# Edge coefficients made beside the propagation instead of beside the counting, in a two-layer graph network on one core

## The chip, the core and the metric

The kernel runs on one core of one Trainium2 chip. TensorE (PE) multiplies; VectorE (DVE), ScalarE (ACT) and GpSimd (POOL) work element by element; SyncE (SP) and POOL issue the transfers. Each engine takes its instructions in program order, and engines wait for one another through semaphores. The metric is the time of one execution in microseconds, the median of the runs.

## The reference

The input is a graph of 3125 nodes with 128 features and 50,000 edges sorted by `dst`. Two graph layers follow one another, each on the normalized features and added to them.

```python
h = relu(layernorm(x)) @ W_in + b_in
deg = segment_sum(ones, row);  w = deg^-1/2[row] * deg^-1/2[col]      # row = src, col = dst
cur = acc = h
for _ in range(3):                                                    # propagation
    cur = segment_sum(cur[col] * w, row);  acc = acc + cur
x = x + (acc / 4) @ W_out + b_out

W_rel = einsum('rb,bio->rio', w_comp, weight)                         # 64 edge types from 16 bases
msg = (relu(layernorm(x)) @ W_rel[etype])[src] * norm
x = x + relu(segment_sum(msg, dst) + h_bias + relu(layernorm(x)) @ loop_weight)
```

For the second layer an edge needs 16 coefficients: the row of `w_comp` for its type, times its `norm`. These are the edge coefficients of the title.

## The kernel before, in words

**Set-up (to 54 us).** Edges lie in 391 tiles of 128, and nodes in 200 windows of 16. A pair is one tile in one window; there are 590 pairs, taken ten at a time in 59 turns. Small tables, made from `dst`, tell each engine what belongs to a turn: `tab_count` holds four words a turn for PE (which PSUM bank each pair adds into, and how many banks must have come free), `tab_end` the pair with which a window ends, in 16 bits.

**Counting (54 to 316 us)** builds the 3200 x 3200 matrix of edge counts, `CT`. For each half turn (five pairs) DVE writes one-hot rows of the edges into one of three half buffers (`onehots`, L757 for five pairs at once and L762 for each). PE multiplies them, pair by pair, into a ring of six PSUM banks, one for each open window (`count_pairs`, L1000). Before it starts a group of pairs (3, 2, 3 and 2 of a turn) it waits for the one-hots and for banks. ACT copies two finished windows at a time to `stage` (L1235) and clears the banks (L1237, `copy_windows`); SP sends them to `CT`. In the last ten turns PE also adds up degrees from finished parts of `CT` (`add_degrees`).

The first 49 turns each also make the coefficients of eight tiles: POOL loads their types, spread over the partitions, into one of three buffers `cbuf` (L520); DVE turns them into one-hots of the type (`type_rows`, L727); PE multiplies with `wc_parts`, `w_comp` in three bf16 parts (L1008); DVE sums the three parts (`sum_parts`, L733) and multiplies by `norm` (`finish_coefs`, L741); POOL stores the result to DRAM (L531). These steps stand between the pairs of the turn on DVE and PE.

**Propagation (321 to 486 us)** has three layers of 25 groups of nodes, a group being 25 products of 128 x 128 with 128 x 192 (L1079). Groups are taken in six blocks of 5, 5, 5, 4, 4 and 2. PE works ahead: it may start a block when DVE has read the block before last out of PSUM (`prop_read`). DVE's chain for a block (L845 to L853, then `thirds`, L808 to L811) reads the sums, scales them and writes the operands of the next layer. In layer 3 the products with `W_out` and the second normalization follow (`between_blocks`).

**Second layer (498 to 985 us)**: POOL gathers a tile of rows at a time (L565), DVE makes operands (L881, L884) from coefficients and rows, PE adds up pairs (L1155, `sum_pairs`) and closes groups (L1135). **End**: PE turns the results back, DVE adds `x2` in seven parts (`add_x2`, L899), SP stores.

The order on every engine is written out by hand; there is no scheduler.

Of the kernel before, what the change touches and what calls it, by code (L numbers as in the profile page):

```python
# [41 lines left out]
P = 128  # L42
# [30 lines left out]
GROUPS = ((0, 3), (3, 5), (5, 8), (8, 10))  # L73
FREE_SHIFT, FREE_MASK = 9, 0xFF
# [3 lines left out]
COEF_MM = 6  # L78
COEF_TYPES, COEF_SUM, COEF_OUT = 4, 7, 9
# [13 lines left out]
CT_TURNS = -(-NT // CCH)  # L93
H_TURNS = -(-NG // 4)
# [63 lines left out]
def build(nc, x, src, dst, etype, norm, W_in, b_in, W_out, b_out, weight, w_comp, h_bias, loop_w, out):  # L158
    assert TURNS * U == S
    ctx = ExitStack()  # L160
    with ctx:
# [19 lines left out]
        tab_count = sb("tab_count", [1, TURNS, len(GROUPS)], I32)  # L181
# [13 lines left out]
        coef_sum = sb("coef_sum", [P, CCH * BASES], F32)  # L195
        coef_out = sb("coef_out", [P, HALVES, CCH * BASES], F32)
# [7 lines left out]
        tab_end = sb("tab_end", [1, NW // 2], U16)  # L204
# [13 lines left out]
        cbuf = rings[:, half:half + HALVES * CHALF].rearrange("p (b e) -> p b e", b=HALVES)  # L218
# [18 lines left out]
        mv2 = carve_keys(NG * 2).rearrange("p (g k) -> p g k", g=NG)  # L237

# [29 lines left out]
        words = carve(TURNS * len(GROUPS))  # L268
# [79 lines left out]
        coef_st = [sem(f"coef_st{b}") for b in range(HALVES)]  # L348
# [48 lines left out]
        def _(sp):  # L397
# [53 lines left out]
            for b in range(NB):  # L451
                if b == NB - 2:
# [4 lines left out]
                    for b3 in range(HALVES):  # L457
                        sp.wait_ge(coef_st[b3], 16 * ((CT_TURNS + 2 - b3) // HALVES))
# [39 lines left out]
        def _(pool):  # L498
# [14 lines left out]
            for u in range(U):  # L513
                pool.memset(weights[:, 0, u:u + 1], float(1 << BANK_BITS * (u % HU % 3))).then_inc(pool_c, 1)
                pool.memset(weights[:, 1, u:u + 1], float(1 << BASE + u - 1) if u else 0.0).then_inc(pool_c, 1)

            def load_types(c, b):
                lo = c * (CCH * P)
                span = slice(lo, lo + CCH * P) if isinstance(c, int) else ds(lo, CCH * P)
                pool.dma_start(cbuf[:, b, :], types_dram[span].rearrange("(h e) -> h e", h=2).unsqueeze(0)  # L520
                               .broadcast_to([TYPES, 2, CHALF])).then_inc(et_in[b], 16)

            def reload_types(c, b):
                pool.wait_ge(coef_mm, c - (HALVES - 1))
                load_types(c, b)

            def store_coefs(c, b):
                pool.wait_ge(coef_cp, c + 1)
                at = c * (CCH * BASES)
                span = slice(at, at + CCH * BASES) if isinstance(c, int) else ds(at, CCH * BASES)  # L530
                pool.dma_start(coef_dram[:, span], coef_out[:, b]).then_inc(coef_st[b], 16)  # L531

            pool.wait_ge(types_st, 16)
            for c in range(HALVES):
                load_types(c, c)
            reload_types(HALVES, 0)
            assert (CT_TURNS - 1 - HALVES) % HALVES == 0
            pool.addr_align(BLOCK, offset=0, max_nops=0)
            with pool.Fori(0, (CT_TURNS - 1 - HALVES) // HALVES) as q:
                for j in range(HALVES):  # L540
                    reload_types(q * HALVES + (j + 1 + HALVES), (j + 1) % HALVES)
                    store_coefs(q * HALVES + j, j)
            for c in range(CT_TURNS - HALVES, CT_TURNS + 1):
                store_coefs(c - 1, (c - 1) % HALVES)


            pool.wait_ge(prop_done, 1)
            pool.memset(wout2[:], 0.0).then_inc(out_zero, 1)
# [33 lines left out]
        def _(dve):  # L582
# [97 lines left out]
            word_of = lambda i: words[0:1, :].rearrange("p (n i) -> p n i", i=2)[:, :, i]  # L680
            for i, (lo, hi) in enumerate(GROUPS[0:2]):
                step(dve.tensor_reduce(word_of(i), halves_of(moved[:, 0])[:, :, lo:hi], AX.X, ALU.add), i == 1)
            for i, (lo, hi) in enumerate(GROUPS[0:2]):
                step(dve.scalar_tensor_tensor(word_of(i), halves_of(ws_s)[:, :, hi - 1], float(1 << FREE_SHIFT), word_of(i),
                                              ALU.mult, ALU.add), i == 1)
            step(dve.tensor_single_scalar(tab_count[:].rearrange("p c i -> p (c i)"), words[0:1, :],
# [38 lines left out]
            def type_rows(c, b, loaded):  # L725
                dve.wait_ge(et_in[b], loaded)
                dve.tensor_scalar(cbuf[:, b, :], cbuf[:, b, :], typ[:, 0:1], None, ALU.is_equal).then_inc(typed, 1)  # L727

            def sum_parts(c):
                dve.wait_ge(coef_mm, c + 1)  # L730
                if not (isinstance(c, int) and c == 0):
                    dve.wait_ge(coef_cp, c)
                dve.tensor_reduce(coef_sum[:], ps[:, COEF_BANK, 0:CCH * BASES * PARTS].rearrange("p (n k) -> p n k", k=PARTS),  # L733
                                  AX.X, ALU.add).then_inc(coef_read, 1)

            def finish_coefs(c, b, stored):
                dve.wait_ge(coef_read, c + 1)
                if stored is not None:
                    dve.wait_ge(coef_st[b], stored)
# [6 lines left out]
            def onehots(c, phase, loaded=None, stored=None, coefs=True):  # L746


                for u in range(U):
# [15 lines left out]
                    if u == COEF_SUM and coefs:  # L765
                        sum_parts(c - 1)
# [586 lines left out]
```

## Time and profile before

| | us |
|---|---|
| median of 3 runs | 1008.39 (1006.3 to 1008.63) |
| the profiled execution | 1009.44 |
| its span, first to last instruction | 1007.9 |
| busy in the span: PE / DVE / POOL / ACT | 810.3 / 738.4 / 446.9 / 356.8 |
| mean granted TensorE clock | 0.93 of full |

The rows further down are from the one profiled execution. In a timeline a row is a run of like instructions: start, time covered, engine, line, operation, output and input, count, and in brackets the idle time before it with what ended it. A row of the table by stretches gives the stretch, for each engine its busy time and, in brackets, the number of instructions, then the granted clock of TensorE as a share of full, the share of the DMA engines and GB/s.

### The profile page before, as it was taken

The page shows a single profiled execution, that of the slowest core. Times are in us where ns is not written, and L with a number is a line of the kernel's source. Part 1 is how long each engine was busy: PE and PEld are TensorE (multiplying, and loading weights), DVE is VectorE, ACT ScalarE, POOL GpSimd, SP SyncE. Part 2 cuts the span into 40 slices and gives each one's busy share as a digit, 9 for nine tenths or more (in the row PEclk, how much of TensorE's full clock was granted, in tenths as well). Part 3 has the DMA queues.
Part 4 walks back from the last instruction along what each step waited for, and adds up shares of the span by engine and source line. Part 5 has one row for each costly group of instructions (what it writes and reads, how often), then busy time and mean ns, then how long its engine had stood idle before and what let it go on. Part 6 is the DMA issues. An engine that isn't in the chain of part 4 may idle for free.

```text
span 1007.9 us, 27188 instructions
## 1 busy us (share of the span) xinstructions
PE 810.3 (80%) x5578; PEld 586.0 (58%) x5583; DVE 738.4 (73%) x2438; ACT 356.8 (35%) x708; POOL 446.9 (44%) x532
## 2 busy tenths in 40 slices
PE   4776777667898999999349889988888888888876
PEld 2622232222455999999237667666666666555544
DVE  7879999999764463534437777777677877887884
ACT  0503457788883000002224454444343332222100
POOL 2013322223100000011277777777777777777771
PEclk8689989999876999999659999999999999999999
DMA  4013345566431000012771111111111111111112
GB/s 120 1 39 82 106 113 132 140 151 154 118 104 51 2 2 1 5 35 85 237 209 52 52 52 54 52 53 52 52 52 52 52 53 54 52 52 52 52 53 77
DMA packets 64848, 73.26 MB, mean 73 GB/s; under 512 B 12803, under 2 KB 53178, under 8 KB 64666
## 3 DMA queue, kind: packets, MB, share of 16 engines
q1 hardware_dynamic: 48362, 37.30, 13.6%
q0 software_dynamic: 16432, 35.29, 12.5%
q8 instruction: 27, 0.44, 0.2%
q14 instruction: 27, 0.22, 0.1%
HBM read 43.85 MB, written 8.22 MB: 52 GB/s over the span
## 4 chain that ended last, share of the span: by engine, by line
PE 36%; DVE 23%; issue 15%; DVEq 9%; POOL 8%; DMA 7%; ACT 2%; SPq 1%; ACTq 0%; POOLq 0%
PE ps L1079 15%; PE ps L1155 10%; POOL CT L565 8%; DMA CT<-h_dram,src_col 5%; PE ps L1000 5%; DVE ohbuf L762 5%; DVE CT L881 5%; DVE CT L884 3%; DVEq L884 3%; DVE u L762 2%; DVEq L124 2%; PE ps L1135 2%; DVE coef_sum L733 2%; DVEq L881 2%; DVE ohbuf L757 1%
## 5 line engine op out<-in xcount | busy, mean ns | idle before, releaser
L565 POOL DMA_INDIRECT CT<-h_dram,src_col x391 | 370.1, 947 | 125.0 <-issue 97.2
L1155 PE MATMUL ps<-CT 128*128 128x256 f32 x1180 | 305.9, 409 | 64.9 <-DVE CT L884 31.7
L1155 PEld LDWEIGHTS ps<-CT 128*128 128x128 f32 x1180 | 206.5, 194 | 158.8 <-issue 140.3
L884 DVE SCALAR_TENSOR_TENSOR CT<-ps,dlP,CT 128x256 f32<-128x256 f32 x580 | 279.9, 483 | 4.3
L881 DVE COPY CT<-CT 128x128 f32 x590 | 148.4, 252 | 124.8 <-PE ps L1155 55.4
L1296 ACT COPY CT<-ps 128x256 f32<-128x256 f32 x200 | 77.7, 388 | 311.2 <-PE ps L1155 297.6
L1000 PE MATMUL ps<-ohbuf 128*128 128x400 bf16 x395 | 118.5, 381 | 37.0 <-DVE ohbuf L762 14.2
L1235 ACT CAST stage<-ps 128x800 bf16<-128x800 f32 x100 | 82.3, 823 | 93.7 <-PE ps L1000 93.3
L520 POOL DMA_DIRECT2D u<-types_dram x49 | 32.5, 668 | 179.3 <-PE ps L1008 166.2
L1079 PE MATMUL ps<-u,CT 128*128 128x192 bf16 x1250 | 105.3, 247 | 0.9 <-DVEq L848 0.9
L1079 PEld LDWEIGHTS ps<-u,CT 128*128 128x128 bf16 x1250 | 103.5, 98 | 2.2 <-DVEq L848 1.1
L762 DVE TENSOR_SCALAR ohbuf<-iota,keys 128x400 bf16<-128x400 int16 x395 | 102.3, 322 | 0.0
L1135 PE MATMUL ps<-CT 128*128 x800 | 95.8, 277 | 6.8 <-ACT CT L1296 4.6
L1135 PEld LDWEIGHTS ps<-CT 128*128 128x128 f32 x800 | 91.2, 192 | 16.7 <-issue 16.7
L1000 PEld LDWEIGHTS ps<-ohbuf 128*128 128x128 bf16 x395 | 39.1, 99 | 105.5 <-issue 82.7
L1237 ACT COPY ps<-zeros 128x800 f32<-128x800 f32 x100 | 83.0, 830 | 8.7
L1000 PE MATMUL ps<-u 128*128 128x400 bf16 x195 | 57.1, 362 | 28.8 <-DVE ohbuf L762 17.2
L1299 ACT COPY ps<-zeros 128x256 f32<-128x256 f32 x200 | 75.2, 376 | 6.4
L553 POOL TENSOR_TENSOR ohbuf<-ohbuf,keys 128x640 f32<-128x640 f32 (+2 forms) x6 | 7.8, 1312 | 143.3 <-DMA ohbuf<-x 143.3
L1256 ACT ACTIVATE keys<-ps 128x256 f32<-128x256 f32 (+1 forms) x6 | 2.2, 365 | 158.2 <-PE ps L1053 158.2
L1000 PEld LDWEIGHTS ps<-u 128*128 128x128 bf16 x195 | 18.8, 96 | 60.8 <-issue 50.8
L845 DVE COPY stage<-ps 128x320 f32<-128x320 f32 (+2 forms) x18 | 7.8, 436 | 63.0 <-PE ps L1079 62.4
(175 smaller groups left out, 671.9 us busy)
## 6 DMA issues: line engine op xcount, KB each, us to landing
CT<-stage SPq DMA_DIRECT2D x200, 100.0 KB, 3.2
u<-types_dram POOLq DMA_DIRECT2D x49, 128.0 KB, 3.4
CT<-h_dram,src_col POOLq DMA_INDIRECT x391, 2.5
coef_dram<-coef_out POOLq DMA_DIRECT2D x49, 64.0 KB, 3.6
CT<-coef_dram SPq DMA_DIRECT2D x1, 3048.0 KB, 12.2
out<-CT SPq DMA_DIRECT2D x4, 256.0 KB
ohbuf<-x SPq DMA_DIRECT2D x3, 320.0 KB, 4.5
x_dram<-ohbuf SPq DMA_DIRECT2D x3, 320.0 KB, 2.3
```

Of the source, the lines that this page charges most:

```text
L565: pool.indirect_dma_start(out=gring[:, (j + 1) % GRING, :], out_offset=None, in_=h2_dram, in_offset=bass.IndirectOffsetOnAxis(ap=src_col[: ...
L762: dve.tensor_scalar(ohB[h][:, u % HU, :], iota16[:], loP[:, col], None, ALU.is_equal).then_inc(oh_ready, 1)
L881: dve.tensor_copy(gpair[:, u:u + 1, :], gring[:, ds(pairs.place(total, GRING), 1), :]).then_inc(pair_in, 1)
L884: dve.scalar_tensor_tensor(kpair[:, u, :, :], nodes.unsqueeze(1).broadcast_to([P, BASES, WIN]), dl, coef_flat[:, ds(tiles * -BASES + NT * ...
L1000: pe.matmul(bank_of(count_words[at], u - lo), ohA[h][:, u % HU, :], ohB[h][:, u % HU, :], start=False, stop=True, skip_group_check=True).t ...
L1079: ins = pe.matmul(psf[:, at:at + PART], CT[:, k, m * P:(m + 1) * P], u[:, k, :], start=(k == 0 and not onto_zeros), stop=(k == NG - 1), sk ...
L1135: pe.matmul(bank, wrel[:, b, :], rows, start=(b == 0), stop=False)
L1155: pe.matmul(ps[:, ds(summed.place(counts[u][0], RING), 1), 0:WIN * BASES], gpair[:, u, :], kpair[:, u, :, :].rearrange("p b d -> p (b d)") ...
L1235: act.copy(stage[:, 2 * i:2 * i + 2, :], ps[:, bank:bank + 2, 0:LO]).then_inc(staged, 1)
L1237: act.copy(ps[:, bank:bank + 2, 0:LO], zeros[:].unsqueeze(1).broadcast_to([P, 2, LO])).then_inc(slots_free, 2)
L1296: act.copy(zsb[:, half, :, j * WIN:(j + 1) * WIN], ps[:, bank, 0:WIN * BASES].rearrange("p (b d) -> p b d", b=BASES)).then_inc(zcopied, 1)
L1299: act.copy(ps[:, bank, 0:WIN * BASES], zeros[:, 0:WIN * BASES]).then_inc(slots2, 1)
```

## The change

1. The coefficient steps leave the counting turns. They now stand in the propagation: POOL waits for the first scaled rows (`u_ready`) and loads three buffers; `COEF_PLAN` says how many of the 49 coefficient turns stand beside which block of which layer. PE puts up to two coefficient products behind each of a block's last groups (`coefs_after`). DVE cuts types (`type_rows`) and sums parts (`sum_parts`) behind the chain of the block before (`coefs_beside`). The product with `norm` moves from DVE to POOL, where it stands ahead of the load for the third turn after it and of its own store. The buffers move into the free part of `stage`, and there are two PSUM banks for the products instead of one.
2. PE's words for a turn: two (for five pairs each) instead of four. PE waits once for each half turn.
3. `tab_end` is 32 bits wide, and ACT masks each value in a register.
4. Of the last `x2` additions and transposes, five are dealt out between the pairs of the last turn instead of ahead of it.

```diff
-GROUPS = ((0, 3), (3, 5), (5, 8), (8, 10))
+COEF_PLAN = {(0, 2): 3, (0, 3): 4, (0, 4): 4, (0, 5): 2, (1, 0): 6, (1, 1): 6, (1, 2): 6, (1, 3): 4, (1, 4): 4, (1, 5): 2,
+             (2, 0): 6, (2, 1): 2}
...
             pool.wait_ge(types_st, 16)
-            for c in range(HALVES):
-                load_types(c, c)
...
-                    reload_types(q * HALVES + (j + 1 + HALVES), (j + 1) % HALVES)
-                    store_coefs(q * HALVES + j, j)
...
+            pool.wait_ge(u_ready, 1)
+            for t in range(HALVES):
+                load_types(t)
             pool.memset(wout2[:], 0.0).then_inc(out_zero, 1)
+            for t in range(CT_TURNS):
+                b = t % 2
+                pool.wait_ge(coef_read, t + 1)
+                if t >= 2:
+                    pool.wait_ge(coef_st[b], 16 * (t // 2))
+                pool.tensor_tensor(coef_out[:, b].rearrange("p (h i b) -> p i h b", h=2, b=BASES),
...
+                                   .broadcast_to([P, CCH // 2, 2, BASES]), ALU.mult).then_inc(coef_cp, 1)
+                if t + HALVES < CT_TURNS:
+                    pool.wait_ge(coef_mm, t + 1)
+                    load_types(t + HALVES)
+                pool.wait_ge(coef_cp, t + 1)
+                pool.dma_start(coef_dram[:, t * CCH * BASES:(t + 1) * CCH * BASES], coef_out[:, b]).then_inc(coef_st[b], 16)
...
-                    if u == COEF_TYPES and loaded is not None:
-                        type_rows(c, phase, loaded)
-                    if u == COEF_SUM and coefs:
-                        sum_parts(c - 1)
-                    if u == COEF_OUT and coefs:
-                        finish_coefs(c - 1, (phase - 1) % HALVES, stored)
...
+            def types_upto(t):
+                while coef_made[0] < min(t, CT_TURNS):
+                    type_rows(coef_made[0])
+                    coef_made[0] += 1
+
+            def coefs_beside(layer, b):
+                for _ in range(COEF_PLAN.get((layer, b), 0)):
+                    types_upto(coef_made[1] + 2)
+                    sum_parts(coef_made[1])
+                    coef_made[1] += 1
+
             for layer in range(LAYERS):
+                coefs_beside(layer, 0)
                 for b in range(NB):
                     got = layer * NB + b
+                    if (layer, b + 1) in COEF_PLAN:
+                        types_upto(coef_made[1] + 2)
                     dve.wait_ge(prop_done, layer * NG + STARTS[b + 1])
...
+                    coefs_beside(layer, b + 1)
...
-            for i in range(len(OUT_PARTS) - 1):
+            operands(TURNS - 1, nodes=iota16[:, 0:WIN], between=add_x2)
+            for i in range(HU, len(OUT_PARTS)):
                 add_x2(i)
-            operands(TURNS - 1, nodes=iota16[:, 0:WIN])
-            add_x2(len(OUT_PARTS) - 1)
...
+            def coef_products(t):
+                if t >= 2:
+                    pe.wait_ge(coef_read, t - 1)
+                pe.wait_ge(typed, t + 1)
+                for i in range(CCH // 2):
+                    n = 2 * BASES * PARTS
+                    last = pe.matmul(ps[:, 6 + t % 2, i * n:(i + 1) * n], cbuf[:, t % HALVES, i * P:(i + 1) * P],
+                                     wc_parts[:].rearrange("p h b k -> p (h b k)"), start=True, stop=True)
+                last.then_inc(coef_mm, 1)
...
+            def coefs_after(layer, b, done):
+                n = COEF_PLAN.get((layer, b), 0)
+                first = 0 if (layer, b) == (LAYERS - 1, 1) else SIZES[b] - (n + 1) // 2
+                for _ in range(max(0, min(2, n - 2 * (done - first))) if done >= first else 0):
+                    coef_products(next(coef_turn))
```

On PE, the second block of layer 2 stood before as 125 products in one piece:

```order
L1079 MATMUL ps<-ohbuf,CT 128x192 [waits prop_read]
L1079 MATMUL ps<-ohbuf,CT 128x192 x124
```

Now the same block reads as follows (L1075 is a group's products, L997 a coefficient product; `typed` comes from DVE's cutting of types, `coef_read` from its sums).

```order
L1075 MATMUL ps<-ohbuf,CT 128x192 [waits prop_read]
L1075 MATMUL ps<-ohbuf,CT 128x192 x74
L997 MATMUL ps<-wc_parts,stage 128x96 [waits typed,coef_read]
L997 MATMUL ps<-wc_parts,stage 128x96 x3
...
L1075 MATMUL ps<-ohbuf,CT 128x192 x25
```

Six waits for DVE now stand in the block, two behind the third group, two behind the fourth and two behind the fifth; the groups behind them are queued.

On DVE, in the same place, coefficient turns stand between the chain of one block and the chain of the next. L728 sums parts of a turn, L721 cuts the types of the turn two further on, and L829 begins the next chain. `et_in0` to `et_in2` are the loads of the three type buffers.

```order
L728 TENSOR_REDUCE keys<-ps 128x128 [waits dve_c,coef_cp,coef_mm]
L721 TENSOR_SCALAR stage<-stage,typ 128x512 [waits et_in0]
L728 TENSOR_REDUCE stage<-ps 128x128 [waits coef_cp,coef_mm]
L721 TENSOR_SCALAR stage<-stage,typ 128x512 [waits et_in1]
L728 TENSOR_REDUCE keys<-ps 128x128 [waits coef_cp,coef_mm]
L721 TENSOR_SCALAR stage<-stage,typ 128x512 [waits et_in2]
...
L829 COPY stage<-ps 128x320 [waits prop_done]
```

Before, nothing stood between one chain and the next here. Now six sums and six cuts do.

On POOL a coefficient turn is three steps in a row (L535 multiplies by `norm`, L521 loads types, L543 stores).

```order
L535 TENSOR_TENSOR coef_out<-stage,norm_col 128x4x2x16 [waits coef_st0,coef_read]
L521 DMA stage<-types_dram 128x1x512 [waits coef_mm]
L543 DMA coef_dram<-coef_out 128x128 [waits coef_cp]
L535 TENSOR_TENSOR coef_out<-keys,norm_col 128x4x2x16 [waits coef_st1,coef_read]
```

The load of a turn's types, which before waited for PE's product alone, now stands behind the multiplication of the turn three before it, and that one waits for DVE's sum.

## Rows read from the trace of the kernel before

**Rows 1.** Busy time by stretch of counting: PE, PEld, DVE, ACT, POOL, clock, DMA, GB/s.

```profile
58.00:150.00 92.00, 65.67 (x308) 27.10 (x308) 88.99 (x326) 34.75 (x42) 29.23 (x43) 0.93 0.34 91
150.00:200.00 50.00, 34.96 (x168) 14.54 (x168) 49.94 (x183) 35.62 (x44) 13.96 (x24) 0.94 0.54 135
200.00:250.00 50.00, 34.94 (x169) 14.31 (x167) 49.50 (x181) 41.32 (x52) 15.63 (x25) 0.95 0.66 153
250.00:307.00 57.00, 48.81 (x580) 25.88 (x581) 38.69 (x141) 47.30 (x59) 3.59 (x3) 0.80 0.42 110
```

**Rows 2.** Timeline of DVE in counting, a turn with coefficients: its first one-hots, the next turn's.

```profile
77.46 0.49 DVE L757 TENSOR_TENSOR ohbuf<-iota,keys 128x640 bf16<-128x640 int16 x1
...
81.52 0.49 DVE L757 TENSOR_TENSOR u<-iota,keys 128x640 bf16<-128x640 int16 x1
```

**Rows 3.** The same of a turn without coefficients.

```profile
259.49 0.49 DVE L757 TENSOR_TENSOR ohbuf<-iota,keys 128x640 bf16<-128x640 int16 x1 [0.23 <-issue]
...
262.63 0.49 DVE L757 TENSOR_TENSOR ohbuf<-iota,keys 128x640 bf16<-128x640 int16 x1
```

**Rows 4.** Timeline of PE in counting: three turns begin with x3.

```profile
79.18 0.77 PE L1000 MATMUL ps<-ohbuf 128*128 128x400 bf16 x3 [0.69 <-DVE ohbuf L762]
80.15 0.56 PE L1000 MATMUL ps<-ohbuf 128*128 128x400 bf16 x2 [0.20 <-DVE ohbuf L762]
80.90 0.56 PE L1000 MATMUL ps<-ohbuf 128*128 128x400 bf16 x2 [0.20 <-issue]
...
83.67 0.77 PE L1000 MATMUL ps<-u 128*128 128x400 bf16 x3 [1.11 <-DVE u L762]
...
87.70 0.77 PE L1000 MATMUL ps<-ohbuf 128*128 128x400 bf16 x3 [0.70 <-ACT ps L1237]
```

**Rows 5.** Groups by line and form: busy us, mean ns of one, idle before.

```profile
L733 DVE TENSOR_REDUCE coef_sum<-ps 128x128 f32<-128x384 f32 x49 | 27.2, 555 | 0.1
L1008 PE MATMUL ps<-wc_parts,u 128*128 128x96 bf16 x196 | 17.7, 217 | 0.0
L727 DVE TENSOR_SCALAR u<-u,typ 128x512 bf16<-128x512 bf16 x49 | 17.2, 350 | 0.0
L553 POOL TENSOR_TENSOR ohbuf<-ohbuf,keys 128x640 f32<-128x640 f32 x3 | 4.6, 1536 | 117.7 <-DMA ohbuf<-x 117.7
L553 POOL TENSOR_TENSOR ohbuf<-ohbuf,keys 128x256 f32<-128x256 f32 x1 | 0.7, 722 | 6.9 <-DMA ohbuf<-x 6.9
```

**Rows 6.** Type loads: all 49 of L520, then the four between 54 and 70 us.

```profile
DMA to landing us min/median/max: 2.7/3.4/4.1
...
u<-types_dram POOLq DMA_DIRECT2D x4, 128.0 KB, 3.1
```

**Rows 7.** Coefficient stores, all 49 of L531.

```profile
DMA to landing us min/median/max: 2.1/3.6/4.7
```

**Rows 8.** Timeline of DVE in layer 2: first and last of a chain, next chain.

```profile
384.22 0.49 DVE L845 COPY stage<-ps 128x320 f32<-128x320 f32 x1 [6.93 <-PE ps L1079]
...
388.93 0.49 DVE L811 TENSOR_TENSOR u<-stage,u 128x320 bf16<-128x320 f32 x1
394.53 0.49 DVE L845 COPY stage<-ps 128x320 f32<-128x320 f32 x1 [5.11 <-PE ps L1079]
...
413.09 0.42 DVE L845 COPY stage<-ps 128x256 f32<-128x256 f32 x1 [3.05 <-PE ps L1079]
...
416.95 0.43 DVE L811 TENSOR_TENSOR u<-stage,u 128x256 bf16<-128x256 f32 x1
421.34 0.42 DVE L845 COPY stage<-ps 128x256 f32<-128x256 f32 x1 [3.97 <-PE ps L1079]
```

**Rows 9.** Timeline of PE behind the propagation: three products after a wait.

```profile
494.04 1.49 PE L1116 MATMUL ps<-zeros 128*128 128x512 bf16 x3 [4.20 <-DVEq L832]
```

**Rows 10.** Timeline of DVE at the end: first additions, first operands of the last turn.

```profile
986.13 1.29 DVE L899 TENSOR_TENSOR CT<-CT,ps 128x512 f32<-128x512 f32 x2 [2.06 <-PE ps L1178]
...
990.73 0.23 DVE L881 COPY CT<-CT 128x128 f32 x1 [0.58 <-issue]
```

More of the change, by code:

```diff
@@ L267, in build @@
         sixth_i = carve(S).bitcast(I32)
-        words = carve(TURNS * len(GROUPS))
+        words = carve(TURNS * 2)
         tidx_i = carve(TC).bitcast(I32)
@@ L347, in build @@
         coef_cp = sem("coef_cp")
-        coef_st = [sem(f"coef_st{b}") for b in range(HALVES)]
+        coef_st = [sem(f"coef_st{b}") for b in range(2)]
         passed = sem("passed")
@@ L456, in _ @@
                     sp.dma_start(hb[:], h_bias.unsqueeze(1)).then_inc(ld_two, 16)
-                    for b3 in range(HALVES):
-                        sp.wait_ge(coef_st[b3], 16 * ((CT_TURNS + 2 - b3) // HALVES))
+                    for half in range(2):
+                        sp.wait_ge(coef_st[half], 16 * ((CT_TURNS + 1 - half) // 2))
                     sp.dma_start(coef[:, NT - U:NT, :].rearrange("p t b -> p (t b)"),
@@ L865, in _, with operands @@
             pairs = Turn(dve, "pair", NT)
-            def operands(c, first=False, nodes=ps[:, IOTA_BANK, 0:WIN]):
+            def operands(c, first=False, nodes=ps[:, IOTA_BANK, 0:WIN], between=None):
                 row = slice(TURNS - 1 - c, TURNS - c) if isinstance(c, int) else ds(c * -1 + (TURNS - 1), 1)
@@ L887, in operands @@
                                              ALU.is_equal, ALU.mult).then_inc(pair_in, 1)
+                    if between is not None and u % 2 == 1:
+                        between(u // 2)
             operands(0, first=True)
@@ L1157, in sum_pairs @@
                               skip_group_check=True).then_inc(pairs2, 1)
+                    if between is not None and u % 2 == 1:
+                        between(u // 2)
             def complete_groups():
@@ L1187, in _ @@
             assert OUT_PARTS[-2][0] * WPG >= U
-            for i in range(len(OUT_PARTS) - 1):
-                turn_back(i)
-            sum_pairs(TURNS - 1)
+            turn_back(0)
+            turn_back(1)
+            assert len(OUT_PARTS) == HU + 2
+            sum_pairs(TURNS - 1, between=lambda pair: turn_back(pair + 1) if pair else None)
             pe.reg_alu(done_reg, groups_reg, 31, ALU.bitwise_and)
```

153 lines of the change are left out of this document (59 added, 94 removed).

## The prediction

> **What bounds the kernel now.** I read the table by stretches first, then the timelines of DVE and PE in a stretch where nobody rests, then the groups by line, and last the transfers.
>
> In counting, DVE is busy 89.0 of 92, 49.9 of 50 and 49.5 of 50 us up to 250 us, ACT only 34.8, 35.6 and 41.3 [rows 1]. So DVE sets the pace there. From 250 to 307 us it is busy 38.7 of 57, while ACT has 47.3 and PE 48.8; there the ring of banks, ACT's copies and the degree sums hold the turn. A turn with coefficients takes DVE 81.52 - 77.46 = 4.06 us [rows 2], one without 262.63 - 259.49 = 3.14 [rows 3]. In propagation PE is the bound: the reader is to see that DVE waits 6.93, 5.11, 3.05 and 3.97 us ahead of its chains [rows 8], and that five groups take 394.53 - 384.22 = 10.31 us, so 2.06 a group, and a block of four 421.34 - 413.09 = 8.25. DVE's chain for a block of five lasts from 384.22 to 389.42, 5.2 us, for one of four 4.3 [rows 8]. The change thus takes work from a stage where DVE is full and puts it where DVE rests about half the time. The question is whether it can be done there as a side job.
>
> **Counting: -34 us.** DVE sheds 4.06 - 3.14 = 0.92 us in each of 49 turns, 45 us in all; that is the most that can be won. What is late next is PE. Its turns begin at 79.18, 83.67 and 87.70 [rows 4]: 4.49 and 4.03 us. Inside a turn, two pairs and the gap to the next piece take 80.90 - 80.15 = 0.75; a piece of three covers 0.77 and one of two 0.56, so a pair costs 0.21, and the gap between pieces adds 0.75 - 2 x 0.21 = 0.33. Two of the three inner gaps go with the two words, 0.66, and the coefficient products, about 0.2. That leaves 3.63 and 3.17; a loop of three turns has one of the longer kind, so 3.3 on the mean, a little above DVE's 3.14. By stretches [rows 1]:
> - 58 to 150: 92 x (1 - 3.3/4.06) = -17.
> - 150 to 200: 50 x 0.187 = -9, to 41; ACT's 35.6 still fit.
> - 200 to 250: PE would come to 41 too, but ACT has 41.3 of its own and must be handed finished windows; I take 44.5, -5.5.
> - 250 to 307: ACT's 47.3 leave little; -2.5.
>
> Sum -34. Bounds: -45 (all that DVE sheds), and -17 if the long turn starts of PE stay (3.63 us for every turn up to 200 us, 142 x 0.106 = 15, and little after). The wait for five pairs at once lets PE start a half turn only when banks for all its windows are free; this takes from the late stretches and is in the 44.5. The mask on ACT is a register step; two of them, with the waits, fit into PE's gap of 0.33, so at most some 0.15 x 100, hidden while ACT waits; I count nothing. The set-up's few steps fewer I count at nothing too.
>
> **Propagation: +64 us.** The 196 products cost PE little: 17.7 us busy at the most [rows 5], at 0.25 a turn 12. What costs is the ring of dependent steps behind three type buffers. DVE's order is sum t, cut t+2, sum t+1, cut t+3, sum t+2. Cut t+3 needs a load that POOL issues only behind its multiplication of turn t, and that needs sum t. So two turns can't be shorter than this ring:
> - sum 0.56 and cut 0.35 on DVE [rows 5];
> - POOL's multiplication of 128 elements: no row has one so small. 640 take 1.54 us and 256 take 0.72 [rows 5], which is 0.0021 us an element and 0.18 fixed: 0.45. Bounds: 0.31 (a fifth of the row of 640) and 0.72;
> - the load, issue to landing: 3.1 in the quiet stretch from 54 to 70 us, 2.7 to 4.1 over all [rows 6]. Propagation is quiet too, so 3.1;
> - four handoffs, some 0.25.
>
> Together 4.7 us for two turns. The chain of a block comes on top, since DVE does nothing for coefficients during it, and the last cut ahead of it (t+7 behind six turns) waits for its own load. A block of five with six turns takes 3 x 4.7 + 5.2 = 19.3 us instead of 10.3; one of four with four turns 2 x 4.7 + 4.3 = 13.7 instead of 8.25. PE can't run ahead of this: its next groups are queued behind products that wait for `typed`, and DVE gives that only behind the chain. The stalls of PE should be 2 to 4 us each, two or three a block.
> - four blocks with six turns: 4 x 9.0 = 36
> - four with four: 4 x 5.45 = 22
> - the two blocks of two groups, two turns each, at the same 1.4 us a turn: 5.5
> - the three turns of the first block lie where DVE rests and with buffers already full, and this also spares most of the next block's excess, about -5; the last two turns and the delayed rest of the ring at the end give about as much back. Zero.
>
> Sum 64. With loads of 2.7 us it is 24.5 x 0.4 = 10 less, with 4.1 us 24 more; with 2.1, the fastest coefficient store [rows 7] as the nearest row below, 24 less. POOL's bounds give -3 and +7. So 37 to 95. The coefficient stores (two buffers) come due two turns later, 4.7 us or more; the slowest landed in 4.7 [rows 7], so they hold nothing.
>
> One rule speaks against the 3.1. The Trainium skill ("DMA: Bandwidth & Descriptors", section on the anatomy of a DMA from GpSimd) gives about 2.0 us fixed plus bytes by 436 GB/s; for 128 KB my estimate from that page is 2.3 us, and the sum would be 24.5 x 0.8 = 20 smaller, +44. The row has no load that fast, so the row decides.
>
> **End: -2.5 us.** DVE now waits 2.06 us for the first transposes [rows 10] and makes the last turn's operands from 990.73 on. After, operands begin where the wait was and five of seven additions go between them; what the wait held, and an addition behind the last pairs, come off. Bounds 0 and -4.
>
> **Sum.** The profiled execution, 1009.44 us: -34 + 64 - 2.5 gives 1037. The median of before lies 1.05 lower, so 1036 by median; I say 1036.
>
> **The rivals.**
> - *The side job keeps up (faster).* The loads run far enough ahead that PE waits for nothing and only its 12 us remain: 1009.4 - 34 + 12 - 2.5 = 985. For it: DVE rests 3 to 7 us a block [rows 8]. Against it: six turns a block need 1.7 us a turn with DVE's chain in the way, and the ring gives 2.35 without the chain. It decides in favour of faster from an excess below 36 us, which by 24.5 x (3.1 - load) needs loads under 2.0 us; none was seen. 9 in 100.
> - *Quicker loads, the ring still rules.* With loads of 2.3 us, between the fastest store's 2.1 [rows 7] and the fastest load's 2.7 [rows 6], 64 - 24.5 x 0.8 = 44, so 1016. For it: with so little other traffic loads may land sooner than at 54 to 70 us. Against: all 49 took 2.7 or more. 15 in 100. The Trainium skill's figure above would give the same.
> - *PE loses its clock.* Stalls of several us, then products at the lower level of 1.2 GHz. For it: after a wait of 4.20 us three products of 512 columns took 1.49 us [rows 9], which is that level. Against: the stalls here are shorter and come between whole groups, and 25 products of 192 columns in 2.06 us are the full level of 2.4 GHz. A group would take 4.1; a block with six turns 5 x 4.1 + 3 = 23.5 instead of 19.3, one with four 18.4 instead of 13.7; if it holds half of the time, (4 x 4.2 + 4 x 4.7) / 2 = 18: 1054. The Trainium skill ("TensorE: Matmul & The Clock Gate", section on oscillation) describes this for products that wait for transfers every few us; no row of propagation shows it yet. 14 in 100.
> - *Counting gives half.* PE's turn starts stay long: -17, 1053. 8 in 100.
>
> **How the numbers follow.** The forecast has 54 in 100, with 1022 to 1050 as its own range. The range for 8 in 10 goes from 1007, which leaves out the side job that keeps up and the fastest loads, to 1064, which takes in clock or counting but not both with slow loads. About 0.3%, 3 us, is what a measurement of this kernel tells from no change. Slower by more: forecast, clock, counting, and most of the quicker loads, 0.85. Faster: 0.11, the rest 0.04.
>
> **What would show it.** In the profile after: counting ends near 282 us instead of 316; DVE's one-hot turns come every 3.2 to 3.4 us; DVE's cuts (L721) wait 2 to 3 us each for loads; PE's L997 waits for DVE 40 to 50 us in all; the stretch of propagation is some 229 us instead of 165; the load of types lands 3 us after its issue. Wrong would be: loads that land in 2 us, cuts that wait for nothing, or a counting stage that hardly shrinks.

## The result, and the profile after

The changed kernel takes 1038.37 us (median of 4 runs, 1036.69 to 1039.11), the kernel before on the same chip 1007.99 (4 runs): ratio 1.0302, 95% interval 1.0282 to 1.0321, slower by 30 us. The profiled execution took 1037.64 us, its span 1035.8.

The sum of the stages in the two profiled spans is made from four moments: PE's first group of the propagation, DVE's cast of `iota` into `ps` behind it (the end of the propagation), the last operands of turn 58 (the last but one), and the end of the span.

| stage | before, us | after, us | difference | predicted |
|---|---|---|---|---|
| up to the first group | 320.76 | 298.39 | -22.4 | -34 |
| propagation | 173.60 | 228.96 | +55.4 | +64 |
| gather to turn 58 | 489.23 | 487.96 | -1.3 | 0 |
| end | 24.31 | 20.49 | -3.8 | -2.5 |
| span | 1007.9 | 1035.8 | +27.9 | +27.5 |

The windows of the changed kernel over counting, with the columns of [rows 1]:

```profile
58.00:150.00 92.00, 61.81 (x259) 24.86 (x259) 82.51 (x308) 44.25 (x54) 0.00 (x0) 0.98 0.22 58
150.00:200.00 50.00, 31.77 (x137) 12.92 (x136) 44.80 (x168) 43.85 (x55) 0.00 (x0) 1.00 0.42 111
200.00:250.00 50.00, 35.19 (x273) 16.66 (x272) 39.09 (x144) 44.01 (x55) 0.00 (x0) 0.90 0.44 115
250.00:307.00 57.00, 46.40 (x655) 31.70 (x656) 30.01 (x95) 30.38 (x39) 2.39 (x4) 0.67 0.29 77
```

DVE is full no longer: 82.5 of 92 us where it had 89.0. ACT has 44 of 50 us from 150 to 250 us, which is nearly as much as it can: its cast and its clearing copy come round every 1.67 to 1.70 us for most of it, and it waits for PE only 6.8 of the 100 us. The timelines of PE and of DVE in one stretch (answering [rows 2 to 4]) show who has taken DVE's place earlier:

```profile
97.21 1.19 PE L988 MATMUL ps<-ohbuf 128*128 128x400 bf16 x5 [0.91 <-DVE u L743]
98.56 1.16 PE L988 MATMUL ps<-ohbuf 128*128 128x400 bf16 x5 [0.17 <-DVE u L748]
100.99 1.20 PE L988 MATMUL ps<-u 128*128 128x400 bf16 x5 [1.26 <-DVE ohbuf L748]
102.35 1.19 PE L988 MATMUL ps<-ohbuf 128*128 128x400 bf16 x5 [0.16 <-issue]
```

```profile
96.71 0.48 DVE L743 TENSOR_TENSOR u<-iota,keys 128x640 bf16<-128x640 int16 x1
97.11 1.25 DVE L748 TENSOR_SCALAR u<-iota,keys 128x400 bf16<-128x400 int16 x5
98.56 0.49 DVE L743 TENSOR_TENSOR ohbuf<-iota,keys 128x640 bf16<-128x640 int16 x1 [0.21 <-PE ps L988]
```

The half in `u` is ready at 98.36 and PE takes it at 100.99; DVE waits at 98.56 for a buffer that PE has just left. So PE is late, and not for one-hots, although the row names DVE as the last releaser. Between 95 and 106 us PE's turns last 3.4 to 3.8 us, 3.55 on the mean, where the prediction had 3.3.

In the propagation, DVE's waits between 298 and 528 us (us in all, times, longest):

```profile
DVE stage L721 <- DMA stage<-types_dram: 53.7, 34, 2.7
DVE stage L829 <- PE ps L1075: 19.8, 5, 10.0
DVE keys L728 <- PE ps L997: 2.5, 5, 0.8
```

The cuts wait for types 34 times in 49, and the chain (L829) waits for PE five times only, ahead of the first coefficients and behind the last. For the coefficient products the sums (L728) wait 2.5 us in all. DVE, which rested ahead of its chains before [rows 8], now holds PE. The timeline of DVE over one block of five with six turns, from one chain's start to the next:

```profile
385.01 0.48 DVE L829 COPY stage<-ps 128x320 f32<-128x320 f32 x1
...
390.43 0.56 DVE L728 TENSOR_REDUCE keys<-ps 128x128 f32<-128x384 f32 x1 [0.22 <-DVE u L779]
390.90 0.34 DVE L721 TENSOR_SCALAR stage<-stage,typ 128x512 bf16<-128x512 bf16 x1
391.16 0.55 DVE L728 TENSOR_REDUCE stage<-ps 128x128 f32<-128x384 f32 x1
394.37 0.35 DVE L721 TENSOR_SCALAR stage<-stage,typ 128x512 bf16<-128x512 bf16 x1 [2.66 <-DMA stage<-types_dram]
394.64 0.55 DVE L728 TENSOR_REDUCE keys<-ps 128x128 f32<-128x384 f32 x1
...
398.48 0.35 DVE L721 TENSOR_SCALAR stage<-stage,typ 128x512 bf16<-128x512 bf16 x1 [1.70 <-DMA stage<-types_dram]
398.79 0.56 DVE L728 TENSOR_REDUCE keys<-ps 128x128 f32<-128x384 f32 x1
...
402.91 0.48 DVE L829 COPY stage<-ps 128x320 f32<-128x320 f32 x1
```

From chain to chain 17.9 us, where it had been 10.3 [rows 8] and was forecast as 19.3. POOL in the same block:

```profile
395.27 0.41 POOL L535 TENSOR_TENSOR coef_out<-keys,norm_col 128x128 f32<-128x128 f32 x1 [1.12 <-DVE keys L728]
395.63 0.58 POOL L521 DMA_DIRECT2D stage<-types_dram  x1
```

The ring can be read off the two fences: sum at 394.64, multiplication 395.27, load issued 395.63, cut 398.48, next sum of its kind 398.79. That is 4.15 us for two turns. PE in the same block waits for the cut, and then runs slowly for a while (in the window below the granted clock is 0.91):

```profile
387.51 2.23 PE L1075 MATMUL ps<-ohbuf,CT 128*128 128x192 bf16 x25
...
394.87 0.48 PE L997 MATMUL ps<-wc_parts,stage 128*128 128x96 bf16 x4 [3.15 <-DVE stage L721]
395.15 3.44 PE L1075 MATMUL ps<-ohbuf,CT 128*128 128x192 bf16 x25
398.42 0.34 PE L997 MATMUL ps<-wc_parts,stage 128*128 128x96 bf16 x4
```

```profile
321.00:398.00 77.00, 60.72 (x705) 58.90 (x703) 46.72 (x113) 0.00 (x0) 34.84 (x69) 0.91 0.18 58
```

The end, on DVE (answering [rows 10]): the operands of the last turn begin without waiting for a transpose, and the first addition follows behind two pairs.

```profile
1016.34 0.30 DVE L866 COPY CT<-CT 128x128 f32 x1 [0.55 <-PE ps L1155]
...
1017.78 0.69 DVE L886 TENSOR_TENSOR CT<-CT,ps 128x512 f32<-128x512 f32 x1 [0.23 <-PE ps L1180]
```

### The profile page after: what moved, and what is told of

Its sections match the earlier page's. It is cut to its first block, busy times and chain, and to the rows that moved or that the text cites. A ratio compares the mean times of both kernels' runs of the same rounds, so it can differ in the third digit from the quotient of the medians.

```text
span 1035.8 us, 26594 instructions
## 1 busy us (share of the span) xinstructions
PE 798.4 (77%) x5582; PEld 587.0 (57%) x5583; DVE 733.2 (71%) x2387; ACT 355.6 (34%) x708; POOL 457.4 (44%) x581
## 4 chain that ended last, share of the span: by engine, by line
PE 34%; DVE 22%; issue 15%; DMA 10%; DVEq 9%; POOL 7%; ACT 2%; SPq 1%; POOLq 0%; ACTq 0%
PE ps L1155 12%; PE ps L1075 8%; PE ps L988 7%; POOL CT L562 6%; DMA stage<-types_dram 5%; DVE CT L866 5%; DMA CT<-h_dram,src_col 4%; DVE ohbuf L748 4%; PE ps L1135 3%; DVE CT L869 2%; DVEq L869 2%; DVEq L126 2%; DVE u L748 2%; DVEq L748 2%; DVEq L866 1%
## 5 line engine op out<-in xcount | busy, mean ns | idle before, releaser
L866 DVE COPY CT<-CT 128x128 f32 x590 | 150.5, 255 | 123.3 <-PE ps L1155 59.6
L521 POOL DMA_DIRECT2D stage<-types_dram x49 | 29.8, 613 | 293.5 <-DVEq L780 293.5
L988 PE MATMUL ps<-ohbuf 128*128 128x400 bf16 x395 | 99.8, 369 | 43.3 <-DVE ohbuf L748 14.7
L1075 PE MATMUL ps<-u,CT 128*128 128x192 bf16 x1250 | 109.0, 249 | 3.2 <-DVEq L780 1.9
L1075 PEld LDWEIGHTS ps<-u,CT 128*128 128x128 bf16 x1250 | 104.8, 99 | 5.1 <-DVEq L780 2.1
L748 DVE TENSOR_SCALAR ohbuf<-iota,keys 128x400 bf16<-128x400 int16 x395 | 98.9, 319 | 0.0
L988 PE MATMUL ps<-u 128*128 128x400 bf16 x195 | 48.5, 358 | 28.3 <-DVE ohbuf L748 24.0
L1075 PE MATMUL ps<-ohbuf,CT 128*128 128x192 bf16 x625 | 60.7, 263 | 2.3 <-DVEq L780 1.9
L1075 PEld LDWEIGHTS ps<-ohbuf,CT 128*128 128x128 bf16 x625 | 57.0, 105 | 3.4 <-DVEq L780 2.1
L743 DVE TENSOR_TENSOR ohbuf<-iota,keys 128x640 bf16<-128x640 int16 x79 | 38.6, 489 | 24.9 <-PE ps L988 24.6
```

Of the source, the lines that this page charges most:

```text
L748: dve.tensor_scalar(ohB[h][:, u % HU, :], iota16[:], loP[:, col], None, ALU.is_equal).then_inc(oh_ready, 1)
L866: dve.tensor_copy(gpair[:, u:u + 1, :], gring[:, ds(pairs.place(total, GRING), 1), :]).then_inc(pair_in, 1)
L988: pe.matmul(bank_of(word, u % HU), ohA[h][:, u % HU, :], ohB[h][:, u % HU, :], start=False, stop=True, skip_group_check=True).then_inc(pai ...
L1075: ins = pe.matmul(psf[:, at:at + PART], CT[:, k, m * P:(m + 1) * P], u[:, k, :], start=(k == 0 and not onto_zeros), stop=(k == NG - 1), sk ...
```

## The experiments

"Propagation" is measured as in the table above, in the profiled execution. Medians of runs that were made on one chip stand beside that chip's median of before: 1007.99 for the change, 1009.8 for the four below it, 1008.67 for the next four, 1008.39 for the last four.

| kernel | us | ratio to before, interval | propagation, us |
|---|---|---|---|
| after | 1038.37 | 1.0302, 1.0282 to 1.0321 | 229.0 |
| load ahead of the multiplication | 1025.54 | 1.0156, 1.0138 to 1.0175 | 217.4 |
| no type loads | 996.36 | 0.9867, 0.9846 to 0.9889 | 186.0 |
| no coefficient steps | 983.57 | 0.9742, 0.9724 to 0.9760 | 172.9 |
| before, with the end alone | 1005.86 | 0.9957, 0.9941 to 0.9974 | - |
| loads by SP | 1005.77 | 0.9974, 0.9961 to 0.9988 | 194.8 |
| after, four groups on PE | 1055.76 | 1.0469, 1.0455 to 1.0483 | 229.2 |
| before, packed words alone | 1010.90 | 1.0014, 1.0000 to 1.0029 | 173.3 |
| after, words loaded early | 1035.67 | 1.0277, 1.0263 to 1.0291 | 230.5 |
| load ahead, stores by ACT | 1011.18 | 1.0025, 1.0013 to 1.0038 | 202.4 |
| loads by SP, words early | 1002.51 | 0.9949, 0.9936 to 0.9962 | 194.2 |
| the same, stores by ACT | 1000.82 | 0.9926, 0.9911 to 0.9941 | 196.8 |
| the same, four type buffers | 990.89 | 0.9831, 0.9818 to 0.9843 | 183.1 |

### What the coefficients cost in propagation, and what of it is the load

Two kernels leave work out. The first drops every coefficient step there (shown is DVE's part; those of PE and POOL go too):

```diff
...
-                for _ in range(COEF_PLAN.get((layer, b), 0)):
+                for _ in range(0):
                     types_upto(coef_made[1] + 2)
...
```

> The changed kernel without the coefficient steps in propagation: no type loads, cuts, products, sums and multiplications; ones are stored in their place (the coefficients are not those of the reference). Every theory expects propagation to be as long as before, 173 us, and the whole 1038 - 55 = 983, if the trace's split into counting -22, propagation +55, gather and end -5 is right. If the longer propagation hid something else (other placement of buffers, stores), it stays above 990.

It takes 983.57 us, and propagation 172.9, as before the change. So the 55 us are the coefficients and nothing else that moved. The second keeps all but the loads:

```diff
-                dve.wait_ge(et_in[t % HALVES], 16 * (t // HALVES + 1))
+                if t < HALVES:
+                    dve.wait_ge(et_in[t % HALVES], 16)
+                else:
+                    dve.wait_ge(coef_mm, t - HALVES + 1)
...
-                if t + HALVES < CT_TURNS:
-                    pool.wait_ge(coef_mm, t + 1)
-                    load_types(t + HALVES)
```

> The changed kernel with the type loads of turns 3 to 48 left out: the cuts run over what lies in the three buffers (the coefficients are not those of the reference), waiting only for the products that read the buffer before. All products, cuts, sums, multiplications and stores stay. Theory: without the load's 2.8 us a two-turn ring is cut, products and handoffs, under 1.2 us, and of the 55 us by which propagation is longer only the products (12) and what DVE's chains hold up (some 5 to 10) stay: 17 to 22, so 1000 to 1006. Rival A (work): 1035 to 1038. Rival B (clock): the products keep coming without stalls, so as the theory.

It takes 996.36, somewhat less than the theory's 1000 to 1006, far from rival A. Propagation is 186.0: of the 55.4 us, 43 stand behind the loads and 12.4 are left, about the products' 12. So DVE's 49 sums and cuts and POOL's multiplications cost next to nothing by themselves, though DVE waits 6.7 us for POOL in that trace. The loads' 43 include what PE loses to its clock behind the waits, since the granted clock is 1.00 in this kernel from 321 to 475 us.

### Where the load stands in the ring

```diff
             for t in range(CT_TURNS):
                 b = t % 2
+                if t + HALVES < CT_TURNS:
+                    pool.wait_ge(coef_mm, t + 1)
+                    load_types(t + HALVES)
                 pool.wait_ge(coef_read, t + 1)
...
-                if t + HALVES < CT_TURNS:
-                    pool.wait_ge(coef_mm, t + 1)
-                    load_types(t + HALVES)
```

> The changed kernel with POOL issuing the type load of turn t+3 ahead of its multiplication of turn t (it waits only for the products of turn t). Theory (the ring through the multiplication and the load sets the pace of propagation): sum, multiplication and two handoffs, some 1.2 us, leave the ring of two turns, 24.5 times, so about -25 to -30 us: 1008 to 1014. Rival A (the work itself: products on PE, cuts and sums on DVE): no instruction is removed, so 1038 within 3. Rival B (TensorE's clock after stalls): stalls shrink but groups behind them stay at the lower level, 1025 to 1035.

A miss: 1025.54, some 13 us less than the change instead of 25 to 30. The direction is the theory's, but something else came due. The time lies in the range of rival B, so its mechanism has to be looked for: the busy time of the groups' products in the changed kernel, in this one and, for comparison, in the kernel with SP's loads further down, whose granted clock is 1.00 from 321 to 475 us.

```profile
L1075 PE MATMUL ps<-u,CT 128*128 128x192 bf16 x1250 | 109.0, 249 | 3.2 <-DVEq L780 1.9
L1075 PE MATMUL ps<-ohbuf,CT 128*128 128x192 bf16 x625 | 60.7, 263 | 2.3 <-DVEq L780 1.9
```

```profile
L1075 PE MATMUL ps<-u,CT 128*128 128x192 bf16 x1250 | 106.8, 246 | 3.6 <-DVEq L780 1.8
L1075 PE MATMUL ps<-ohbuf,CT 128*128 128x192 bf16 x625 | 57.1, 254 | 2.7 <-DVEq L780 1.8
```

```profile
L1081 PE MATMUL ps<-u,CT 128*128 128x192 bf16 x1250 | 106.8, 246 | 1.3 <-DVEq L838 0.9
L1081 PE MATMUL ps<-ohbuf,CT 128*128 128x192 bf16 x625 | 54.0, 246 | 0.4 <-DVEq L786 0.4
```

That is 169.7, 163.9 and 160.8 us. So the lower clock lengthens PE's work by 8.9 us in the changed kernel and by 3.1 in this one: most of it has gone, and it is not rival B that holds the time up. The timeline of POOL in this kernel names what does:

```profile
387.10 0.59 POOL L543 DMA_DIRECT2D coef_dram<-coef_out  x1 [0.29 <-POOL coef_out L538]
387.68 0.60 POOL L521 DMA_DIRECT2D stage<-types_dram  x1
388.23 0.49 POOL L538 TENSOR_TENSOR coef_out<-stage,norm_col 128x128 f32<-128x128 f32 x1
389.02 0.59 POOL L543 DMA_DIRECT2D coef_dram<-coef_out  x1 [0.29 <-POOL coef_out L538]
389.60 0.60 POOL L521 DMA_DIRECT2D stage<-types_dram  x1
```

In this stretch POOL rests only the 0.29 us that it waits for its own multiplication: a load every 1.92 us (387.68 to 389.60), of which two issues take 0.6 each. Two turns take 3.84 us so, hardly less than the ring's 4.15. The prediction had no term for the time that an issue takes of POOL. Two kernels tell this apart from the load's own latency. In one POOL no longer stores:

```diff
...
-                pool.wait_ge(coef_cp, t + 1)
-                pool.dma_start(coef_dram[:, t * CCH * BASES:(t + 1) * CCH * BASES], coef_out[:, b]).then_inc(coef_st[b], 16)
...
+            for t in range(CT_TURNS):
+                act.wait_ge(coef_cp, t + 1)
+                act.dma_start(coef_dram[:, t * CCH * BASES:(t + 1) * CCH * BASES],
+                              coef_out[:, t % COUT]).then_inc(coef_st[t % COUT], 16)
```

> The kernel with the load moved ahead on POOL, and the coefficient stores issued by ACT, which rests in propagation. Theory (POOL's queue held it: load 0.60, multiplication 0.49, wait for it 0.29 and store 0.59 make 1.92 us a turn; without the store and its wait 1.1): POOL no longer sets the pace, and the time comes near that with SP's loads, 1003 to 1009. Rival (it matters who issues the load, SP being quicker than POOL): it stays at 1018 to 1026.

In the other POOL no longer loads (the first three loads move to SP as well):

```diff
...
+            for t in range(early):
+                sp.wait_ge(coef_mm, t + 1)
+                load_types(t + HALVES)
...
+            for t in range(early, CT_TURNS - HALVES):
+                sp.wait_ge(coef_mm, t + 1)
+                load_types(t + HALVES)
```

> The changed kernel with the type loads issued by SP, which waits for nothing but the products that free the buffer; POOL keeps the multiplications and stores. Theory after the first runs (the load's latency, and POOL's queue of 1.92 us a turn when it issues load and store and multiplies): the cuts find their types nearly always, PE's groups of 2.06 us with two products set the pace, propagation is 12 us longer than before for the products and 4 to 10 for what is left of the stalls: 1000 to 1006. Rival (the latency of 2.7 us alone, whoever issues): as with the load moved ahead on POOL, 1020 to 1025.

1011.18 and 1005.77. The stores taken off POOL are worth 15 us of propagation (217.4 to 202.4), so its queue had taken the ring's place; the time lies 2 us above the range of the theory, and the cuts still wait for loads 27.7 us. With SP's loads propagation is 21 us longer than before instead of 55. The transfer itself is no quicker from SP, as the lists of DMA issues show (KB each, median us from issue to landing), the changed kernel first:

```profile
stage<-types_dram POOLq DMA_DIRECT2D x49, 128.0 KB, 2.8
```

```profile
stage<-types_dram SPq DMA_DIRECT2D x49, 128.0 KB, 2.7
```

What counts is when the load is issued: behind a multiplication and a store, or at once when its buffer comes free. The Trainium skill ("Perfetto Trace Analysis", DMA Optimizations) says that balancing transfers over the engines that can issue them may help where the issuing engine looks full; the 15 us above agree. The Trainium skill's "DMA: Bandwidth & Descriptors" (Issuing engine by pattern) holds the hardware path to be generally faster; for this transfer, 2.7 against 2.8, no run here shows that.

### Packing, with and without the freed DVE

```diff
...
-FREE_SHIFT, FREE_MASK = 12, 0xFF
-LAST_SHIFT = 20
+GROUPS = ((0, 3), (3, 5), (5, 8), (8, 10))
+FREE_SHIFT, FREE_MASK = 9, 0xFF
...
-                    if u % HU == 0:
-                        pe.wait_ge(oh_ready, c * (U + 2) + (u // HU + 1) * (HU + 1))
+                    if u == lo:
+                        pe.wait_ge(oh_ready, c * (U + 2) + (hi + (hi - 1) // HU + 1))
...
```

> The changed kernel with the old four groups of pairs and the old tables on PE and ACT (the packing undone, all else as changed). Theory (in counting PE is what DVE waits for, and the packing is what took two of its gaps away): PE's early turns grow from 3.55 us by two gaps of 0.33 to 4.1 or so, over some 28 turns up to 160 us, and ACT's bound later hides part: +8 to +15, so 1046 to 1053. Rival (the wait of five pairs for banks costs more late than it gives early, 4 us of lead lost in the last turns): 1034 to 1037.

And the reverse, the packed words alone in the kernel before (diff as above with the signs turned, and without the table of ends):

> The kernel before with PE's packed words alone (groups of five pairs; coefficients still made in counting, table of ends as before). Theory (DVE sets the pace there with 4.06 us a turn): nothing early; late the five-pair waits cost up to 4: same to +4, 1009 to 1013. Rival (PE and DVE wait for each other through the one-hot buffers, so a shorter PE turn helps already): -3 to -6.

1055.76 and 1010.90. The first went 17 us up, against 8 to 15 expected. Starts of ACT's casts show where (us; the 33rd, the 79th and the last of 100):

| kernel | 33rd | 79th | 100th |
|---|---|---|---|
| before | 177.13 | 267.95 | 309.72 |
| after | 160.25 | 241.55 | 287.34 |
| after, four groups | 174.60 | 263.97 | 304.99 |
| before, packed words | 176.44 | 266.68 | 313.03 |
| after, words early | 160.02 | 241.53 | 283.62 |

Freeing DVE alone gives 2.5 us by the 33rd cast, packing alone 0.7, both 16.9: as long as one of the two engines has the long turn the other's short one is worth little. Between the 79th cast and the last, both packed kernels lose 4 to 5 us, as the theory of the second had it, and the one with four groups gains 0.7: that loss comes with the packed words. PE's timeline in the changed kernel there:

```profile
277.18 1.49 PE L988 MATMUL ps<-ohbuf 128*128 128x400 bf16 x5 [0.68 <-ACT ps L1242]
278.50 1.39 PE L1014 MATMUL ps<-ones_bf,CT 128*128 128x1 bf16 x50
280.54 1.22 PE L988 MATMUL ps<-u 128*128 128x400 bf16 x5 [0.65 <-ACT ps L1242]
283.44 0.84 PE L988 MATMUL ps<-ohbuf 128*128 128x400 bf16 x2 [1.68 <-ACT ps L1242]
```

Three waits for ACT's clearing copy, 3.0 us, at the start of half turns that need banks for five pairs at once.

### What makes PE's gap at a turn's start

```diff
...
+                    if u == HU and not (isinstance(c, int) and c == TURNS - 1):
+                        load_words(c + 1, (phase + 1) % HALVES)
...
```

> The changed kernel with PE's two words of a turn loaded in the middle of the turn before, into registers of their own (three sets), instead of at the turn's start. Theory (the load of the words is most of PE's 0.9 us gap at a turn's start): some 0.4 us less in each of 28 early turns, -5 to -9, so 1029 to 1033. Rival (the gap is the wait for one-hots and banks and the loop's branch): within 2 of 1038.

1035.67, 2.7 us less by the medians, though the intervals overlap; and not where the theory had it: the 33rd cast starts at 160.02 instead of 160.25. The gap of 0.9 stands as it was, with no load of words ahead of it:

```profile
95.00 1.18 PE L992 MATMUL ps<-u 128*128 128x400 bf16 x5 [0.91 <-DVE ohbuf L743]
96.35 1.16 PE L992 MATMUL ps<-ohbuf 128*128 128x400 bf16 x5 [0.17 <-DVE ohbuf L748]
98.39 1.19 PE L992 MATMUL ps<-ohbuf 128*128 128x400 bf16 x5 [0.88 <-DVE ohbuf L743]
100.13 1.20 PE L992 MATMUL ps<-u 128*128 128x400 bf16 x5 [0.55 <-DVE ohbuf L748]
```

So the load of the words isn't PE's gap of 0.9 in the early turns; what is stays open. In every third turn the gap had been 1.26 or more; that part has come down to 1.0 or less, and in return one half turn in six begins behind a gap of 0.55 where it had 0.17 (100.13). So the longer part of the gap has moved with the load rather than gone. The gain lies behind the 79th cast (the last cast starts at 283.62 instead of 287.34): of the 4 us that the packed words lose there, 0.3 are left. The packed words lose that much only where they are also loaded late; how the wait for five pairs and the late load share it stays open as well.

### The end alone

DVE's part of the edit (PE's transposes are dealt out in the same way):

```diff
...
-            for i in range(len(OUT_PARTS) - 1):
+            operands(TURNS - 1, nodes=iota16[:, 0:WIN], between=add_x2)
+            for i in range(HU, len(OUT_PARTS)):
                 add_x2(i)
-            operands(TURNS - 1, nodes=iota16[:, 0:WIN])
-            add_x2(len(OUT_PARTS) - 1)
```

> The kernel before with the last part alone: the x2 additions dealt out between the operands of the last turn, and the transposes between its pairs. Theory: the end gives 3.8 us as in the trace of the changed kernel, 1008 to 1004. Rival: the end gained only because the gather's last turns came in another rhythm there, so less than 1 us here.

1005.86 against 1009.8: 3.9 us, as in the trace of the changed kernel.

### Towards a version that beats both

> SP's loads and PE's words loaded a half turn ahead, together. The two touch different stages and should add: 1005.8 - 2.7 = 1003. Rival: what counting gives is taken back at its end by the degree sums or the first loads, so 1005.

1002.51, near the 1003 expected. The interval just touches that of SP's loads alone, so the sum is borne out, but not by much.

> The same, and the coefficient stores issued by ACT, with three output buffers instead of two. Theory: DVE's sums wait for POOL's multiplication in each block with six turns (0.4 to 0.5 us at a time, some two a block); without the store POOL needs 0.7 us a turn: -2 to -5 against the kernel without it, so 998 to 1001. Rival: what remains of the stalls is loads alone, so within 1.

1000.82: that lies in the theory's range, 1.7 us below the one before, but the intervals overlap, and propagation in the trace is 2.6 us longer instead of shorter. The trace speaks for the rival, that POOL's store was no bound any more; the times don't decide it.

> The same with a fourth type buffer (in the row of zeros, which is cleared again after the last product). Theory: PE's rest in front of its products (10 us in the kernel with SP's loads) is the load landing after its buffer came free a group earlier; with one buffer more it goes to 2 to 4 us: another -5 to -8, so 992 to 995, the 12 us of products being what stays. Rival: DVE's order (chain, cuts and sums of a block, about 10.6 us of a block's 11.9) holds it: within 2 of the one before.

```diff
...
-        cbuf = spare[:, 0:HALVES * CHALF].rearrange("p (b e) -> p b e", b=HALVES)
+        cbuf = [spare[:, b * CHALF:(b + 1) * CHALF] for b in range(HALVES)] + [zeros[:, 0:CHALF // 2].bitcast(BF16)]
...
+            pool.wait_ge(coef_mm, CT_TURNS)
+            pool.memset(zeros[:, 0:CHALF // 2], 0.0).then_inc(out_zero, 1)
...
```

990.89, 1.7% faster than the kernel before and some 47 us faster than the change; 10 us by the medians are the fourth buffer's, 2 more than its theory's best. PE's timeline over groups with products, and its window (columns as above):

```profile
380.09 2.23 PE L1090 MATMUL ps<-ohbuf,CT 128*128 128x192 bf16 x25
382.15 0.33 PE L1011 MATMUL ps<-wc_parts,zeros 128*128 128x96 bf16 x4
382.65 0.33 PE L1011 MATMUL ps<-wc_parts,stage 128*128 128x96 bf16 x4 [0.16 <-DVE stage L731]
382.81 2.23 PE L1090 MATMUL ps<-ohbuf,CT 128*128 128x192 bf16 x25
```

```profile
317.00:394.00 77.00, 76.41 (x986) 75.97 (x986) 64.14 (x156) 0.00 (x0) 14.49 (x33) 1.00 0.28 85
```

PE is busy 76.4 of 77 us; for the cuts it waits once in the whole propagation, 0.2 us. The side job keeps up here, and propagation is 9.5 us longer than before, about what the products themselves take.

## Why the prediction was right, and what of it was not

The forecast was 1036, the median is 1038, and the mechanism that it named decides: the ring of sum, multiplication, load and cut. But two of its terms were off by some 10 us each, in opposite directions. That the sum came within 2 us is luck; that the kernel is slower is not, since propagation's 55 us are more than twice what counting gives.

- **Counting, -34 against -22.4.** ACT's casts, compared one by one, give the gain at the prediction's own marks, by the clock of the kernel before. The 22nd cast starts at 150.89 before and 137.35 after, the 43rd at 198.97 and 178.88, the 69th at 249.95 and 224.05. So 13.5 us were won up to 150 us (17 forecast), 6.6 up to 200 (9), 5.8 up to 250 (5.5), and 3.5 were lost behind it (2.5 won forecast). In the first two stretches PE's early turn was mis-sized, 3.55 us and not 3.3: its inner gaps went as forecast, to 0.16 to 0.19, but the gaps at turn starts grew, from 0.69, 1.11 and 0.70 [rows 4] to 0.91, 1.26 and 0.89. The stretch where ACT sets the pace was right. The largest miss is the last one, where the packed words lose 4 us behind the 79th cast. The wait for five pairs was named in the text, but only inside another number.
- **Propagation, +64 against +55.4.** The ring is 4.15 us instead of 4.7: the load took 2.85 there (2.8 on the median) and not the 3.1 of [rows 6], the sum with its handoff 0.63, the multiplication with its handoff 0.36, the cut 0.31. The starts of DVE's chains, before and after, share the excess out in the prediction's own terms: 29.9 us for the four blocks with six turns (36 forecast), 19.9 for the four with four (22), 2.5 for the two with two (5.5), and 3.1 for the rest, which the forecast put at zero. Of this rest the three turns of the first block are 4.3 and the last two turns -1.5. So the shorter ring took off some 11 us, and the first block, which was not free, put 3 back.
- **The multiplication on POOL, 0.45**, was 402 to 456 ns. Right, as was the chain that comes on top: 5.4 us from 385.01 to the next sum against 5.2, during which PE can go no further than its cut types.
- **End, -2.5 against -3.8**, inside its bounds; shown by the kernel with the end alone.
- **Rival "the side job keeps up":** not in this kernel, for the reason given; with loads issued at once and a fourth buffer it does. Its 985 and the 12 us that counting gave less make 997; 991 was found, some 3 of it by the words loaded early.
- **Rival "quicker loads":** the load did come down towards it, 2.7 at the least, 2.8 on the median, and so did propagation. None of the 49 reaches the prediction's estimate of 2.3 us from the Trainium skill ("DMA: Bandwidth & Descriptors", anatomy of a DMA from GpSimd).
- **Rival "PE loses its clock":** it does in places. Behind a wait of 3.15 us 25 products took 3.44 instead of 2.23 us, elsewhere 3.88 and 4.20; at the lower of the two levels a group takes 4.1 by the prediction. It lengthens PE's work by 8.9 us in all (169.7 against 160.8), but little of that reaches the time, since DVE's ring rules. In the block shown the second of the two products behind the slow group needed the cut of 398.48 in any case. Over the whole propagation the sums wait 2.5 us for PE's products, and the chains wait for PE only ahead of the first coefficients and behind the last, so the ring can feel no more than those 2.5. No kernel took the clock alone away. In the one with four buffers the granted clock is 1.00 in the window shown.
- **Rival "counting gives half":** it came part of the way. The 22.4 us lie between its 17 and the forecast's 34, and long turn starts, its mechanism, are what the first two stretches show.

Wrong in "what would show it": counting did not end near 282 us but near 294. The cuts waited 1.6 us on the mean, 34 of 49 times, and not 2 to 3 each. PE's products L997 waited 30.1 us, all of it for cuts, where 40 to 50 had been named. The 229 us named for propagation, from the first group to the last chain, are 220; the 229.0 of the tables above run on to the cast of `iota`, and that the two figures agree is chance.

## What to carry to other kernels

Work moved beside another engine's work is a ring of its own: count the turn of that ring with its transfer, and ask what each buffer's load is queued behind, before adding busy times. A load belongs on a queue where nothing stands between the freed buffer and its issue, and with one buffer more than the latency needs; here these two, with the stores on ACT, turned +55 us into +10. Where two engines feed each other, shortening either alone is worth little: up to the 33rd cast the packed words gave 0.7 us alone, the freed DVE 2.5, both together 17.

## What the runs showed of the hardware that was not expected

- An issue on POOL is work: 0.58 to 0.60 us each for the load of 128 KB and the store of 64 KB (medians), so that two of them and a multiplication of 0.49 fill 1.92 us with the wait between them.
- The 128 KB load lands in 2.7 to 2.9 us on the median in every kernel that makes all 49 beside the propagation, whether POOL or SP issues it.
- A wait put down to DVE by the profile (PE at 100.99) need not be one: the half that PE took had been ready for 2.6 us.
